# Two depthwise convolutions around an MLP: 56-column back transposes, another order of the set-up and of the transfers, an early load for the last stage

## The reference

```
y = depthwise_conv7x7(x, dw_w, padding 3) + dw_b            # per channel
y = (y - mean_c) * rsqrt(var_c + 1e-6) * ln_w + ln_b        # over the 96 channels
h = gelu(y @ w1 + b1)                                       # 96 -> 384
gx = sqrt(sum_hw(h*h));  nx = gx / (mean_c(gx) + 1e-6)
h = grn_gamma * (h * nx) + grn_beta + h
z = x + (h @ w2 + b2)                                       # 384 -> 96
w = round_to_power_of_2(clampabs(conv_w, 2**-14, 1))
zq = clip(floor(z * 65536) / 65536, -32768, 32767)
out = depthwise_conv3x3(zq, w, padding 1) + fixed_point(conv_b)
```

## Time and profile before

| | before |
|---|---|
| median of 3 runs | 1080.56 us |
| the profiled execution | 1080.37 us |
| its span, first to last instruction | 1078.6 us |
| mean granted TensorE clock | 0.963 |
| busy: TensorE, ScalarE, VectorE, POOL | 92%, 77%, 77%, 38% |
| bytes moved by DMA | 182.95 MB, 170 GB/s over the span |

### The profile page before, as it was taken

How to read it: one execution, slowest core, us unless ns; L and a number is a source line. 1 busy time by engine, 2 the same in 40 slices (tenths; PEclk the granted TensorE clock), 3 DMA queues, 4 the chain that set the end, 5 groups by cost and what they waited for, 6 DMA issues and landing times.

```text
span 1078.6 us, 21092 instructions
## 1 busy us (share of the span) xinstructions
PE 990.8 (92%) x5574; PEld 717.7 (67%) x5574; DVE 825.5 (77%) x1768; ACT 830.8 (77%) x1724; POOL 411.7 (38%) x353
## 2 busy tenths in 40 slices
PE   3999999999999467999999999999999849999996
PEld 2788888888888355666666666666666427767774
DVE  7777777777777565888888888888887667888885
ACT  2688888888887357898988888888888607787874
POOL 2666676666666153332333333333332001111110
PEclk9999999999999766999999999999999978999999
DMA  8777777777772592555555555555543247999995
GB/s 162 147 183 182 181 179 184 187 187 179 180 179 66 131 225 82 157 175 163 172 162 171 172 162 170 162 171 162 167 136 90 80 110 187 245 248 243 247 244 154
DMA packets 146312, 182.95 MB, mean 170 GB/s; under 512 B 13799, under 2 KB 140424, under 8 KB 143208
## 3 DMA queue, kind: packets, MB, share of 16 engines
q1 hardware_dynamic: 145480, 179.97, 62.5%
q10 hardware_dynamic: 800, 2.61, 1.0%
HBM read 124.28 MB, written 58.25 MB: 169 GB/s over the span
## 4 chain that ended last, share of the span: by engine, by line
PE 71%; DVE 12%; ACT 6%; issue 6%; DMA 3%; DVEq 1%; POOL 0%; ACTq 0%; SPq 0%; POOLq 0%
PE psum L573 22%; PE psum L653 21%; PE psum L643 6%; PE psum L644 6%; PE psum L645 6%; PE psum L552 6%; PE psum L600 3%; DVE arena_r L894 3%; ACT arena L706 2%; ACT arena_r L691 2%; DVE arena L919 1%; DMA arena<-lines_a 1%; DVE arena L923 1%; DVE arena L1079 1%; DVE arena L1068 1%
## 5 line engine op out<-in xcount | busy, mean ns | idle before, releaser
L573 PE MATMUL psum<-arena_r 112*128 112x464 f32 x1536 | 375.2, 386 | 0.3 <-issue 0.2
L573 PEld LDWEIGHTS psum<-arena_r 112*128 112x128 f32 x1536 | 276.8, 190 | 33.9 <-issue 1.1
L653 PE MATMUL psum<-arena,w2s 128*96 128x448 f32 x672 | 266.8, 542 | 2.8 <-DVE w2s L994 2.8
L787 ACT ACTIVATE arena<-psum,b1g 128x448 f32<-128x448 f32 x336 | 201.8, 630 | 58.3 <-PE psum L645 58.2
L497 POOL TENSOR_TENSOR arena_r<-arena,arena_r 96x448 fp32r<-96x448 f32 x112 | 134.1, 1197 | 268.7 <-DVE arena_r L969 194.8
L653 PEld LDWEIGHTS psum<-arena,w2s 128*96 128x96 f32 x672 | 109.8, 164 | 119.1 <-issue 111.8
L643 PE MATMUL psum<-arena_r,w1h 96*128 96x448 f32 x336 | 154.1, 459 | 14.2 <-POOL arena_r L497 13.0
L706 ACT ACTIVATE arena<-psum,bias_a 64x224 f32<-64x224 f32 (+1 forms) x288 | 117.0, 442 | 61.8 <-PE psum L573 50.6
L894 DVE TENSOR_TENSOR arena_r<-psum,arena_r 112x224 fp32r<-112x224 f32 x384 | 127.2, 382 | 48.3 <-ACT arena_r L691 47.5
L691 ACT ACTIVATE arena_r<-psum 112x224 fp32r<-112x224 f32 x384 | 112.6, 355 | 54.8 <-PE psum L552 52.5
L486 POOL TENSOR_TENSOR arena<-arena 128x448 f32<-128x448 f32 x96 | 110.0, 1146 | 109.8 <-DVE arena L923 109.2
(11 more groups left out here) (94 smaller groups left out, 1146.1 us busy)
## 6 DMA issues: line engine op xcount, KB each, us to landing
arena<-lines_a SPq DMA_DIRECT2D x48, 448.0 KB
arena<-in_x_dram SPq DMA_DIRECT2D x48, 392.0 KB
y_scratch<-arena SPq DMA_DIRECT2D x48, 392.0 KB
arena<-in_x_dram SPq DMA_DIRECT2D x112, 168.0 KB, 2.5
z_scratch<-arena SPq DMA_DIRECT2D x112, 168.0 KB, 2.0
arena<-z_scratch SPq DMA_DIRECT2D x48, 392.0 KB
out_dram<-arena SPq DMA_DIRECT2D x48, 392.0 KB
arena_r<-y_scratch SPq DMA_DIRECT2D x98, 168.0 KB, 2.6
```

Source lines behind the costliest of these rows:

```text
L573: mm = nc.tensor.matmul(p_conv[s % 2][:, 0:NCOL], w[:, p, s, TW * k:TW * k + TW], v[:, p, s, slot0 + k:slot0 + k + JP, :].rearrange("p j i ...
L653: mm = nc.tensor.matmul(p_o[k][0:C, 0:CH], w2s[:, p, m, :], hid[:, p, m, CH * t:CH * t + CH], start=(m == 0), stop=(m == MT - 1))
L787: nc.scalar.activation(hid[:, p, m, CH * t:CH * t + CH], p_h[m][:, 0:CH], ACT.Gelu, bias=b1g[:, m:m + 1]).then_inc(gelu_done, 1)
```

## The change

1. The line's tap position and the shift of the table reads differ by 8, so that the 56 results of a row lie on partitions 0 to 55 (and 64 to 119) and not on 8 to 63. The back transposes read 56 partitions and write 56 columns; before it was 64. The same goes for the eight transposes of the statistics.
2. The 49 tap copies become one instruction, as do the 9 of the second convolution. It stands right after the halos' clearing and two memsets; the other memsets and constants follow. ScalarE issues the 11 small loads in place of SP and waits for them only before its first `yt_copy`.
3. Batch 0's tables in stage a are loaded channel by channel (8 DMAs), and the convolution waits for its own channel's table.
4. Both stages use one order of transfers: rows and tables of batch b+1, then the store of batch b-2.
5. The MLP's `hid` is split in two, so that the first half (the even images) can be overwritten in the tail. SP loads the rows of images 0 to 13 and the tables of stage c's batch 0 there, ahead of the last image's z stores. Images 14 and 15 follow after the last store. POOL clears the halos once the last `up` is done, and TensorE doesn't wait for the last rounding.

The diff, cut to its core:

```diff
 def forwards(v, n):
-    return bass.AP(tensor=v.tensor, offset=v.offset + LSTEP - 1,
-                   ap=[part, [LSTEP, n], [bank, 2], [-1, W]])
+    return bass.AP(tensor=v.tensor, offset=v.offset + W - 1,
+                   ap=[part, [W, n], [bank, 2], [-1, W]])
...
-        hid = mlp(128, 2, MT, HW)
+        hid = [hid0, mlp(128, MT, HW)]
...
@ load_tables
-                    shifted = bass.AP(tensor=lines, offset=b * (CB * kt * TW) + LPAD + r * LSTEP - (LSTEP - 1),
+                    shifted = bass.AP(tensor=lines, offset=b * (CB * kt * TW) + LPAD + r * LSTEP - (W - 1),
...
@ conv_transfers
                             need(sp, S["tin"], G * b)
                             load_rows(S, src, b + 1, 1 - s)
-                            if ahead:
-                                tables(b + 1, 1 - s)
-                        if not ahead:
-                            tables(b, s)
-                        if not (isinstance(b, int) and b < 3):
-                            store(b - 3, 1 - s)
+                            tables(b + 1, 1 - s)
+                        if not (isinstance(b, int) and b < 2):
+                            store(b - 2, s)
                 bodies(sp, body, 2)
-                for b in range(NBATCH - 3, NBATCH):
+                for b in range(NBATCH - 2, NBATCH):
                     store(b, b % 2)
...
-            tables_a(0, 0)
-            conv_transfers(stages["a"], x_v, y_v, tables_a, True)
+            for k in range(CB):
+                for r in range(2):
+                    shifted = bass.AP(tensor=lines_a, offset=k * (KA * TW) + LPAD + r * LSTEP - (W - 1), ap=[[1, W], [1, KA * TW]])
+                    sp.dma_start(toep[W * r:W * r + W, 0, k, :], shifted).then_inc(t_first[k], 16)
+            conv_transfers(stages["a"], x_v, y_v, tables_a)
...
+            sp.wait_ge(o_done, NCH * (NIMG - 1))
+            for k in range(4):
+                sp.wait_ge(z_out[k], 16 * Z_USES[k % 2] * (NIMG // 2 - 1))
+            first_rows(0, NI2 - 1, c_early)
+            tables_c(0, 0)
             step(NIMG, 0, more_y=False, more_x=False)
             for k in range(4):
                 sp.wait_ge(z_out[k], 16 * Z_USES[k % 2] * NIMG // 2)
-            load_rows(stages["c"], z_v, 0, 0)
-            sp.wait_ge(halo, 2)
-            conv_transfers(stages["c"], z_v, out_v, tables_c, False)
+            first_rows(NI2 - 1, NI2, stages["c"]["x0"])
+            conv_transfers(stages["c"], z_v, out_v, tables_c)
...
@ gpsimd, after its MLP steps
+            pool.wait_ge(h_done, MT * NCH * NIMG)
+            for v in (xt_h, xt_l):
+                for slots in (slice(0, HALO), slice(HALO + NPAIR, SLOTS)):
+                    pool.memset(v[:, :, :, slots, :].bitcast(F32), 0.0).then_inc(halo, 1)
...
@ tensor, convolve
+                    if S is stages["a"]:
+                        pe.wait_ge(S["tl"], n + 1)
                     if s == 0:
-                        if S is stages["a"]:
-                            pe.wait_ge(S["tl"], CB * b + CB)
-                        else:
+                        if S is stages["c"]:
                             pe.wait_ge(S["th"], b + 1)
...
@ tensor, back
-                            mm = nc.tensor.transpose(outs[s % len(outs)][0:CM, 1 - r, LSTEP * n:LSTEP * n + LSTEP],
-                                                     yt[q:q + LSTEP, p, i, (h + 1 - r) % 2].rearrange("p g m -> p (g m)"),
-                                                     ident[q:q + LSTEP, q:q + LSTEP])
+                            mm = nc.tensor.transpose(outs[s % len(outs)][0:CM, 1 - r, W * n:W * n + W],
+                                                     yt[q:q + W, p, i, (h + 1 - r) % 2].rearrange("p g m -> p (g m)"),
+                                                     ident[q:q + W, q:q + W])
...
-            pe.wait_ge(v_ready, NCH * NIMG)
...
@ vector
             link(clear_halos())
+            dve.sem_inc(halo, 1)
+            dve.memset(la, 0.0)
+            link(dve.memset(zrow, 0.0))
+            dve.wait_ge(dw_in, 16)
+            at = LSTEP - 3
+            taps = la[:, at:at + 7 * LSTEP].rearrange("p (y x) -> p y x", y=7)
+            dve.tensor_copy(taps[:, :, 0:7], wa.rearrange("p (y x) -> p y x", y=7)).then_inc(lines_made, 1)
...
-            for dy in range(7):
-                for dx in range(7):
-                    at = (dy + 1) * LSTEP + dx - 3
-                    ins = dve.tensor_copy(la[:, at:at + 1], wa[:, 7 * dy + dx:7 * dy + dx + 1])
-            link(ins)
-            dve.sem_inc(lines_made, 1)
...
-            dve.wait_ge(z_ready, NCH * NIMG)
-            dve.wait_ge(sq_act, 2 * MT * NIMG)
-            link(clear_halos())
-            dve.sem_inc(halo, 1)
```

More of the change, by code:

```diff
@@ L192, in build @@
         yl = mlp_r(C, HW)
+        hid0 = mlp(128, MT, HW)
         ct = mlp(C, 2, CH)
         xr = mlp(C, HW)
-        hid = mlp(128, 2, MT, HW)
         rt = mlp(C, 2, CH).bitcast(I32)
@@ L215, in build @@
         dw_in = sem("dw_in")
+        t_first = [sem(f"t_first{k}") for k in range(CB)]
         consts = sem("consts")
@@ L233, in build @@
         m2_done = sem("m2_done")
+        c_early = sem("c_early")
         var_ready = sem("var_ready")
@@ L324, in _ @@
             load_rows(stages["a"], x_v, 0, 0)
[L325 to L336, removed]
             def store_lines(lines, made, zrow, kt):
@@ L362, in tables_c, with conv_transfers @@
                 load_tables(stages["c"], lines_c, KC, toep_b, b, s)
-            def conv_transfers(S, src, dst, tables, ahead):
+            def conv_transfers(S, src, dst, tables):
                 runs_of = dst.rearrange("(i g) c (m t) -> g (c m) i t", g=2, t=RUN)
@@ L441, in _, with first_rows @@
             step(NIMG - 1, 1, more_y=False)
+            def first_rows(i0, i1, done):
+                rows_of = z_v.rearrange("(i g) c (m t) -> g (c m) i t", g=2, t=RUN)
+                for g in range(2):
+                    sp.dma_start(xin[CR * g:CR * g + CR, 0, i0:i1, :], rows_of[g][0:CR][:, i0:i1]).then_inc(done, 16)
+            sp.wait_ge(o_done, NCH * (NIMG - 1))
[3 more added lines that the diff above has]
+            tables_c(0, 0)
             step(NIMG, 0, more_y=False, more_x=False)
@@ L521, in tables @@
                     pool.sem_inc(tables_turn, 1)
-                    pool.wait_ge(halo, 2)
+                    pool.wait_ge(halo, 5)
                     pool.tensor_copy(toep_h[:, p, :, 0:KC * TW], toep_b[:, p]).then_inc(S["th"], 1)
@@ L545, in tin @@
                     n = G * b + s
-                    if s == 0:
+                    if S is stages["c"] and isinstance(b, int) and b == 0:
+                        if s == 0:
+                            pe.wait_ge(c_early, 32)
+                        if s == G - 1:
+                            pe.wait_ge(S["x0"], 32)
+                    elif s == 0:
                         pe.wait_ge(S[f"x{p}"], 16 * (b - p) + 32)
@@ L633, in _ @@
                     a = LSTEP * (1 - r)
-                    mm = nc.tensor.transpose(p_stat[0:IG * NPAIR, 1 - r, LSTEP * g:LSTEP * g + LSTEP],
-                                             rstd_in[a:a + LSTEP, IG * NPAIR * g:IG * NPAIR * (g + 1)], ident[a:a + LSTEP, a:a + LSTEP])
+                    mm = nc.tensor.transpose(p_stat[0:IG * NPAIR, 1 - r, W * g:W * g + W],
+                                             rstd_in[a:a + W, IG * NPAIR * g:IG * NPAIR * (g + 1)], ident[a:a + W, a:a + W])
             mm.then_inc(stat_t, 1)
@@ L652, in down @@
                 for m in range(MT):
-                    mm = nc.tensor.matmul(p_o[k][0:C, 0:CH], w2s[:, p, m, :], hid[:, p, m, CH * t:CH * t + CH],
+                    mm = nc.tensor.matmul(p_o[k][0:C, 0:CH], w2s[:, p, m, :], hid[p][:, m, CH * t:CH * t + CH],
                                           start=(m == 0), stop=(m == MT - 1))
@@ L678, in _ @@
         def _(act):
-            act.wait_ge(small_in, 16 * NSMALL)
+            for dst, src in ((wc, cw.rearrange("c o h w -> c (o h w)")),
+                             (bias_a[:, :], dw_b.rearrange("(o c) -> o c", o=1).to_broadcast([TW, C])),
+                             (bq[0], cb.rearrange("(o c) -> o c", o=1).to_broadcast([TW, C])),
+                             (w1r, w1),
+                             (b1t[:, :], b1.rearrange("(t p) -> p t", p=128)),
+                             (w2r[:, :, :], w2.rearrange("(t p) c -> p t c", p=128)),
+                             (gam[:, :], grn_gamma.rearrange("(t p) -> p t", p=128)),
+                             (bet[:, :], grn_beta.rearrange("(t p) -> p t", p=128)),
+                             (lnw[:, :], ln_w.rearrange("(p o) -> p o", o=1)),
+                             (lnb[:, :], ln_b.rearrange("(p o) -> p o", o=1)),
+                             (b2c[:, :], b2.rearrange("(p o) -> p o", o=1))):
+                act.dma_start(dst, src, allow_slow_non_contiguous=True).then_inc(small_in, 16)
             act.wait_ge(halo, 1)
@@ L696, in yt_copy @@
```

(19 more changed lines are left out.)

9 lines of the change are left out of this document (2 added, 7 removed).

## The result

The changed kernel takes 1132.59 us, the median of 4 runs (1130.06 to 1133.33), against 1080.58 us for the kernel before on the same chip: the ratio is 1.0477, with a 95% interval of 1.0459 to 1.0495. It is slower, as forecast, but by 52 us and not by 21; the time lies above the range.

What follows compares the result with a forecast made beforehand. TensorE, VectorE's chain and nearly full DMA queues were taken to be close, with transfer order deciding. From 1080.4 us, back transposes -1.2, set-up -1.7, last stage's start -3.7 and store order +28 gave 1101.8 us; range 1073 to 1120.

Steps and rivals of the forecast that it cites:

- What bounds the kernel: Whole kernel: three resources, among them TensorE and the DMA queues, are within a few per cent; transfer order decides which wins.
- Store order, +28: Last stage: rows of b+2 queue behind the store of b-2, +2.8 us a pair over 10 pairs, ends +16 and +36.
- L: Last stage: time from the store's issue until rows b+2 have landed, taken as 8.6 us, between 7.4 and 9.0.
- The clock falls too: Rival, last stage: pauses in every second batch halve the clock, 1.7 us each, ten times, giving 1119 us; chance 0.19.
- The first stage: First convolution stage: the same store order is covered, rows landing 4 us before they are wanted; 0 us.
- The loads land in time: Rival, last stage: below 5.8 us from store issue to rows landed nothing is lost, giving 1073.8 us; chance 0.23.
- Back transposes, -1.2: 56 columns for 64 take 27 ns off a group, 48 first-stage groups on the chain: -1.2 us; last stage 0.
- Set-up, -1.7: Kernel's start: one tap instruction lets the lines be issued at about 3.3 us; -1.7 us, ends 0 and -3.3.
- if those go first, nothing is gained: Set-up: small loads moved to ScalarE share the engines with rows and lines; if they go first, the gain is 0.
- Eight table issues in place of two cost SP 3 us, covered by 0.92 MB in flight: Set-up: the extra issue time on SP is hidden behind 4.5 us of transfers in flight.
- The last stage's start, -3.7: Early load of images 0 to 13 and tables starts the last stage's convolution 0 at 887.9, not 891.63; ends -2.5 and -5.

Runs made afterwards that it cites:

- store3: Changed kernel with both convolution stages storing batch b-3 again, tables still one batch ahead: 1074.54 us, ratio 0.994.
- keep_busy: Changed kernel with 20 unused matmuls of 384 columns ahead of each wait for an even batch's rows in the last stage: 1123.22 us.
- wait_no_store: Changed kernel with rows and tables issued behind the wait for the out copies, but ahead of the store that awaited the same: 1086.31 us.
- back56: Kernel before with the back transposes of 56 columns alone: 1079.17 us, ratio 0.9985.
- lines_on_act: `store3` with SP issuing the 11 small loads after batch 0's rows, and ScalarE storing the taps' lines from its own queue: 1073.78 us, ratio 0.9941.
- small_on_sp: `store3` with SP issuing the 11 small loads again, after batch 0's rows and ahead of the lines: 1074.26 us, ratio 0.9942.
- late_first: `store3` with the last stage's early load undone, all 16 images of batch 0 and its tables issued after the last z store: 1076.27 us, ratio 0.9967.
- half_store: Changed kernel with each last-stage store writing only half of a batch's 0.80 MB: 1114.02 us.

## Why the prediction was wrong in size and right in sign

**What bounds the kernel: right.** That the order of transfers decides the last stage, where TensorE, VectorE and the queue are within a few per cent, is what `store3` against the changed kernel shows.

**Store order, +28: the mechanism right, the size half.** By the prediction's own formula a pair is (E after the rows) + 2.26 + L. Term by term, for the pair shown above:

| term | predicted | measured |
|---|---|---|
| rows landed to E, the end of convolution 3 | 0.75 + 6.42 - 0.35 = 6.82 | 8.38, of which 0.12 before TensorE starts |
| E to the store's issue | 2.26 | 2.25 |
| L, the store's issue to the rows' landing | 8.6 | 9.75 |
| a pair | 17.7 | 20.4 |

The step that failed is "The clock falls too", which I had made a rival, with 0.19, instead of a term. The pause does halve the clock, ten times out of ten, and the trace of `keep_busy` gives it 1.5 us a pair, of which the pair kept 1.3. My argument against it, that others take up part and dense work stands around, had nothing measured behind it, while the earlier trace rows was a row for it: a pause of 1.91 us, 3.4 us at half clock. The Trainium skill, TensorE: Matmul & The Clock Gate, section HAM oscillation — how this bites in real kernels, describes just such a loop, in which each wait for a DMA makes the next piece start at the lower clock; the 0.50 after the 4.32 us wait agrees.

The second is L. I built it from a load that ran alone and the store's rate, 9.0 us, had 7.4 from below by the steady rate, and then took 8.6 between them. It was 9.75. The runs show where the rest went. From the issue of what stands first in the queue to TensorE's first transpose, the median over the waits is 6.7 us with the rows alone (`wait_no_store`), 8.40 behind a store of 0.40 MB and 9.96 behind one of 0.80 MB. So 0.80 MB of store cost 3.2 us, some 250 GB/s, and not the 2.6 us that I had from the 305 GB/s of one window of 2 us; and the rows alone take 0.3 us more in the loop than the 6.4 at its start. These two are the 0.9 us by which 9.96 lies above 9.0. With the clock's 1.5 us and this L, the sum would have been 1080.4 - 6.6 + 55 = 1129 us.

The first stage: that its cover holds is right. A batch takes 13.88 us with either order (13.880 changed, 13.874 in `store3`), and TensorE does not wait for rows there.

**"The loads land in time" (0.23): wrong.** It decided from L = 5.8; L was never under 8 with a store in front, not even with half of one.

**Back transposes, -1.2: the value right by luck, the rule wrong.** `back56` measures -1.6 (-0.6 to -2.6), but a group shrinks by 10 ns and not by 27. By the formula 48 x 10 ns give -0.5; the batch in the first stage went from 13.904 to 13.881 us, which is 0.023 x 24 = -0.55 as well. A batch of the last stage went from 7.457 to 7.445 us, another -0.3, though no back group lies on its lap as I had read it. Together that is -0.85, inside the interval; what the median has beyond that can't be told from the noise of the traces. The Trainium skill, TensorE: Matmul & The Clock Gate, section LDWEIGHTS (loading the stationary operand), has the load go by the stationary operand's columns, 112 in all three; that 64, 56 and 40 columns give 0.367, 0.357 and 0.344 us is nearly what it says, and so is the pace of the pairs, 54 ns with 56 and with 40. I had it, and took the row of the 112-column transposes instead, in which load and moving columns can't be told apart.

**Set-up, -1.7: wrong, it is 0 to +1.** The lines are issued at 3.20 us, as foreseen, and land at 10.35, where 11.23 was before: 0.9 gained of 3.3. Batch 0's rows are in front of them, but that is only part: alone in a queue, in `lines_on_act`, they land at 9.11, so 1.2 us are the place in the queue and the rest is the sharing of the engines. And the small loads on ScalarE's queue now share the engines with these rows, which land at 9.54 in place of 8.16. The chain of waits in the changed kernel:
```profile
3.20 0.34 SPq L331
...
3.90 6.45 DMA lines_a<-arena
...
10.37 0.33 SPq L379
...
13.75 0.39 SPq L324
...
14.18 9.07 DMA arena<-in_x_dram
```
I had named this sharing ("if those go first, nothing is gained") and then taken the middle. The Trainium skill, DMA: Bandwidth & Descriptors, section Queues, rings and completion order, has each DMA engine take turns between the queues that have work for it; the rows' 1.4 to 1.6 us agree with that, and `small_on_sp`, where the same loads stand behind the rows in one queue, has none of it. A second step was "Eight table issues in place of two cost SP 3 us, covered by 0.92 MB in flight". In the chain above they stand at line 379, 3.34 us from 10.37 on, and batch 1's rows, for which TensorE waits, are issued behind them at 13.75 instead of 12.04. In the changed kernel the DMA engines were busy for only 0.45 of that stretch (last but one number):
```profile
10.40:13.70 3.30, 1.22 (x7) 0.85 (x6) 1.10 (x4) 2.38 (x5) 0.00 (x0) 1.00 0.45 141
```
No run takes these issues back by themselves, so their share in the lost gain isn't shown; `small_on_sp` has them too and starts the first convolution 0.5 us earlier than the kernel before.

The first convolution starts at 24.72 us in the changed kernel and at 23.75 in `store3`, whose instructions are the same up to there, so a single trace tells this place only to 1 us; before it was 23.67.

**The last stage's start, -3.7: right.** It measures -4.1 in the changed kernel and -3.9 in `late_first` against `store3`. Convolution 0 starts at 886.16; the timeline, against the earlier trace rows:
```profile
879.67 0.99 PE L562 MATMUL psum<-ident,arena 112*112 112x112 f32 x4 [3.03 <-DMA arena<-z_scratch]
884.74 1.74 PE L562 MATMUL psum<-ident,arena 112*112 112x112 f32 x8 [4.08 <-DMA arena<-z_scratch]
886.16 1.90 PE L583 MATMUL psum<-arena_r 112*128 112x464 f32 x4
```

The best kernels of the study are the changed one with the store of b-3, 1074.5 us, and the two variants of its set-up, 1074.3 and 1073.8, which can't be told from it.

## What to carry to other kernels

In a queue that issues in order, read each load's issue as "after everything that the instructions ahead of it wait for": here one line of order closed a loop of out copy, store, load and transpose that had been open. When such a loop makes TensorE pause, add the halved clock behind each pause as a term with a price, not as a chance. A transfer's time behind others is to be taken from rows, at the rate that the queue holds over many microseconds and not at that of its best two.

## What the runs showed of the hardware that I had not expected

- After each of ten waits of 4.1 to 4.6 us the granted clock was 0.50 for 3.4 us; 20 matmuls of 384 columns ahead of the wait kept it at 1.00 at nine of the ten, and the pair of batches got only 1.3 of 20.4 us faster.
- SP's issue of two row DMAs took 3.27 us behind a store of 0.80 MB and 1.21 us behind one of 0.40 MB (0.9 us at the kernel's start); TensorE got its rows only 1.56 us earlier.
- With 0, 0.40 and 0.80 MB of store in front, 0.80 MB of rows released TensorE 6.7, 8.40 and 9.96 us after the first issue (medians over the waits of `wait_no_store`, `half_store` and the changed kernel).
- Small loads, 11 of them with few bytes, from ScalarE's queue delayed 0.80 MB of rows on SP's queue by 1.4 to 1.6 us; ScalarE's own issues, 0.43 us each on SP, took up to 1.30 us there.
- Pairs of back transposes with a stationary operand of 112 columns followed each other after 56 ns with 64 moving columns, and after 54 with 56 and with 40.
